# A graph layer's edge loop on one Trainium2 core: one stretch of the node table per two blocks, edge lists laid out two blocks to a row

## What is computed

```python
dst = jnp.minimum((6250 * uniform(100000) ** 2.0).astype(int32), 49999)   # then sorted; src permuted alike
row, col = edge_index[0], edge_index[1]                                  # src, dst
msg_in = concatenate([node_features[row], node_features[col]], axis=-1)
h = relu(msg_in @ Wm1 + bm1)
h = relu(h @ Wm2 + bm2)
messages = h @ Wm3 + bm3
agg = segment_sum(messages, col, 6250) / clip(count, 1.0)[:, None]
node_in = concatenate([node_features, agg], axis=-1)
upd = relu(node_in @ Wn1 + bn1) @ Wn2 + bn2
x = layernorm(x + node_features + upd)
```

## Time and profile before

| | |
|---|---|
| device time, median of 3 runs | 1201.61 us (1199.98 to 1201.78) |
| the profiled execution, first to last instruction | 1416.6 us |
| TensorE busy / VectorE / ScalarE / GpSimd | 88% / 69% / 52% / 56% |
| first transpose of the edge loop, last one | 89.4 us, 1308.2 us |
| moved by DMA | 211.42 MB, mean 149 GB/s |

### The profile page before, as it was taken

The page is one execution under the profiler, slowest core; times in us unless marked ns, Lnnn a source line. Parts: engine busy times, 40 slices in busy tenths (PEclk is TensorE's granted clock), DMA queues, the critical chain, the costliest instruction groups (busy, mean ns, idle before and its releaser), DMA issues.

```text
span 1416.6 us, 33766 instructions
## 1 busy us (share of the span) xinstructions
PE 1249.7 (88%) x9614; PEld 1172.0 (83%) x9615; DVE 979.6 (69%) x2072; ACT 740.6 (52%) x1392; POOL 786.5 (56%) x814
## 2 busy tenths in 40 slices
PE   6978888888888888888888889988999989899997
PEld 6868888888888888888888888888888888888886
DVE  6846666766766666766766766767767767777676
ACT  3544555555555555555555555555554555545585
POOL 2166666666666666666666666666666666564000
PEclk9999999999999999999999999999999999999999
DMA  9665555545545555555545555455545454554022
GB/s 308 274 234 156 146 144 151 149 141 151 151 140 150 152 142 147 151 143 147 152 139 150 146 143 151 145 144 152 139 147 151 138 150 144 145 151 142 10 67 86
DMA packets 135605, 211.42 MB, mean 149 GB/s; under 512 B 24247, under 2 KB 102669, under 8 KB 134030
## 3 DMA queue, kind: packets, MB, share of 16 engines
q1 hardware_dynamic: 98030, 108.43, 25.3%
q0 software_dynamic: 37536, 102.55, 25.1%
HBM read 188.09 MB, written 22.80 MB: 149 GB/s over the span
## 4 chain that ended last, share of the span: by engine, by line
PE 80%; issue 12%; DVE 2%; SPq 1%; another core or an unknown queue 1%; DMA 1%; ACT 1%; DVEq 1%; ACTq 0%
PE bank L1437 39%; PE bank L1413 11%; PE bank L1324 6%; PE sums L1345 4%; PE sums L1341 4%; PE sums L1347 3%; PE sums L1349 3%; PE bank L1478 2%; PE sums L1491 1%; PE bank L1234 1%; PE bank L1219 1%; PE bank L1461 1%; PE sums L1219 1%; DMA b_win<-b_table 1%
## 5 line engine op out<-in xcount | busy, mean ns | idle before, releaser
L630 POOL DMA_INDIRECT a_edge<-a_table,src_idx x782 | 767.1, 981 | 457.8 <-remote 268.2
L1437 PE MATMUL bank<-w,h 128*128 128x256 f32 x4692 | 661.4, 283 | 104.9 <-issue 102.1
L1437 PEld LDWEIGHTS bank<-w,h 128*128 128x128 f32 x4692 | 596.5, 188 | 119.7 <-issue 118.7
L1106 DVE SCALAR_TENSOR_TENSOR h<-bank,h 128x512 fp32r<-128x512 f32 x391 | 268.7, 687 | 338.4 <-issue 326.7
L732 ACT ACTIVATE h<-bank 128x512 fp32r<-128x512 f32 x391 | 233.8, 598 | 475.3 <-remote 439.2
L721 ACT COPY bank<-b_bc 128x512 f32<-128x512 f32 x391 | 231.5, 592 | 115.2 <-issue 66.7
L1118 DVE SCALAR_TENSOR_TENSOR h_lo<-bank,h_hi 128x512 fp32r<-128x512 f32 x391 | 266.5, 681 | 0.1
L1413 PE MATMUL bank<-ident,a_edge 128*128 128x128 f32 x1564 | 237.4, 274 | 21.1 <-issue 16.6
L740 ACT ACTIVATE h_hi<-bank 128x512 fp32r<-128x512 f32 x391 | 232.6, 595 | 2.8 <-PE bank L1437 2.8
L1413 PEld LDWEIGHTS bank<-ident,a_edge 128*128 128x128 f32 x1564 | 180.3, 140 | 40.5 <-issue 34.2
L1324 PE MATMUL bank<-onehot_t,b_win 128*128 128x256 f32 x782 | 190.3, 325 | 0.0
(11 more groups left out here) (190 smaller groups left out, 682.7 us busy)
## 6 DMA issues: line engine op xcount, KB each, us to landing
b_win<-b_table SPq DMA_DIRECT2D x391, 128.0 KB
rel<-rel_dram SPq DMA_DIRECT2D x196, 128.0 KB
a_edge<-a_table,src_idx POOLq DMA_INDIRECT x782
a_table<-work SPq DMA_DIRECT2D x12, 512.0 KB, 4.6
b_table<-work SPq DMA_DIRECT2D x5, 1024.0 KB
b_table<-h SPq DMA_DIRECT2D x4, 1024.0 KB
f_x<-in_x SPq DMA_DIRECT2D x12, 256.0 KB, 5.2
b_table<-a_edge SPq DMA_DIRECT2D x3, 1024.0 KB, 5.8
```

The source lines that it names most:

```text
L630: pool.indirect_dma_start(a_edge[:, b % R * TB + t, :], None, a_table, bass.IndirectOffsetOnAxis(ap=src_idx[:, b * TB + t:b * TB + t + 1], ...
L1106: dve.scalar_tensor_tensor(h1[:, k % U, 1, :], bank[k % 2][:, :], 0.0, h1[:, k % U, 0, :].bitcast(F32), ALU.max, ALU.subtract).then_inc(s_ ...
L1437: ins = pe.matmul(to, h1[:, j, a, h * EB + t * P:h * EB + (t + 1) * P], w2[:, b, h, :], start=False, stop=(a == 1 and h == KH - 1), skip_g ...
```

## The change

Two blocks share one window, which begins at the lower of their two lowest nodes. `b_win` is loaded once a pair, both blocks' relative numbers are taken from the pair's lowest node, and `far` of a block is counted from there too. In front of the loop the edge lists stand two blocks to a row: rows of 2 x 256 edges, in two column groups instead of four, so the loads and the stores of minima, maxima and relative numbers are fewer and their rows twice as long. VectorE makes the pair's minimum in two places (one on 98 x 2 and one on 1 x 392), and GpSimd's two fills of the padding are twice as wide.

```diff
-        full = E // EB
-        assert (GR - 1) * BG <= full
+        full = E // (2 * EB)
+        assert (GR // 2 - 1) * BG <= full < GR // 2 * BG
         loads = []
         for n in range(2):
-            for g in range(GR):
-                rows = min(full - g * BG, BG)
+            for a in range(GR // 2):
+                rows = min(full - a * BG, BG)
                 if rows:
-                    loads.append((n, g, 0, rows, EB))
-            if E % EB:
-                loads.append((n, GR - 1, rows, 1, E % EB))
+                    loads.append((n, a, 0, rows, 2 * EB))
+            if E % (2 * EB):
+                loads.append((n, GR // 2 - 1, rows, 1, E % (2 * EB)))
...
             def body(i):
-                first = load_words(sp, words_sp, i * U, U, PAD_DST)
-                for k in range(U):
-                    if there(i, k - RB):
-                        sp.wait_ge(s_ex, i * U + (k - RB + (2 if k % 2 == 0 else 1)))
-                    if k % 2 == 0:
-                        sp.dma_start(rel[:, k // 2, :].rearrange("p (b e) -> p b e", b=2),
-                                     rel_dram[bass.ds(i * U + k, 2), :].partition_broadcast(P)
-                                     ).then_inc(s_rc[k // 2], 16)
-                    if there(i, k):
-                        sp.dma_start(b_win[:, k % RB, :].bitcast(F32),
-                                     b_table[bass.ds(first[k] * 2, P), :]).then_inc(s_bw[k % RB], 16)
+                first = load_words(sp, words_sp, i * (U // 2), U // 2, PAD_DST)
+                for c in range(RC):
+                    if there(i, 2 * c - U):
+                        sp.wait_ge(s_ex, i * U + (2 * c - U + 2))
+                    sp.dma_start(rel[:, c, :].rearrange("p (b e) -> p b e", b=2),
+                                 rel_dram[bass.ds(i * U + 2 * c, 2), :].partition_broadcast(P)
+                                 ).then_inc(s_rc[c], 16)
+                    sp.dma_start(b_win[:, c, :].bitcast(F32),
+                                 b_table[bass.ds(first[c] * 2, P), :]).then_inc(s_bw[c], 16)
...
                 if k % 2 == 0:
                     dve.wait_ge(s_rc[k // 2 % RC], nth(i, k, 16))
-                dve.wait_ge(s_bw[k % RB], nth(i, k, 16))
+                    dve.wait_ge(s_bw[k // 2 % RC], nth(i, k, 16))
                 dve.wait_ge(s_g[k % R], nth(i, k, 16 * TB))
...
-                dve.tensor_tensor(far, highest, lowest, ALU.subtract).then_inc(s_rw, 1)
+                dve.wait_ge(s_low, 1)
+                dve.tensor_tensor(far, highest, row_low[0:1, :], ALU.subtract).then_inc(s_rw, 1)
...
-                    expand(b_win[:, k % RB, :], onehot_t[:, k % 2, :], k).then_inc(s_ex, 1)
+                    expand(b_win[:, k // 2 % RC, :], onehot_t[:, k % 2, :], k).then_inc(s_ex, 1)
```

More of the change, by code:

```diff
@@ L184, in gnn_layer @@
         minmax_i = carve(2 * GR).bitcast(I32)
+        pair_low = carve(GR // 2)
         first_quarter = carve(GR).bitcast(I32)
@@ L233, in gnn_layer @@
         s_mm = sem("s_min_max")
+        s_low = sem("s_lowest_of_pairs")
         s_wi = sem("s_min_max_int")
@@ L261, in gnn_layer @@
         s_rc = [sem(f"s_rel_loaded{c}") for c in range(RC)]
-        s_bw = [sem(f"s_b_win_loaded{c}") for c in range(RB)]
+        s_bw = [sem(f"s_b_win_loaded{c}") for c in range(RC)]
         s_bf = sem("s_b_far_loaded")
@@ L476, in _ @@
             sp.wait_ge(s_pad, 2)
-            for n, g, row, rows, edges in loads:
-                at, e0 = (n * GR + g) * EB, (g * BG + row) * EB
+            for n, a, row, rows, edges in loads:
+                at, e0 = (n * GR + 2 * a) * EB, (a * BG + row) * 2 * EB
                 sp.dma_start(edges_in[row:row + rows, at:at + edges],
@@ L516, in _ @@
                     sp.wait_ge(s_wi, 1)
-                    for j in range(GR):
-                        sp.dma_start(mm_dram[j * BG:(j + 1) * BG, :], minmax_i[0:BG, 2 * j:2 * j + 2]
-                                     ).then_inc(s_scr, 16)
+                    for a in range(GR // 2):
+                        sp.dma_start(mm_dram[a * 2 * BG:(a + 1) * 2 * BG, :].rearrange("(p c) m -> p (c m)", c=2),
+                                     minmax_i[0:BG, 4 * a:4 * a + 4]).then_inc(s_scr, 16)
                 if g == 4:
-                    sp.wait_ge(s_scr, 16 * GR)
+                    sp.wait_ge(s_scr, 16 * (GR // 2))
                     sp.dma_start(row_in[0:1, :], mm_dram.rearrange("(o b) c -> o (b c)", o=1)).then_inc(s_row, 16)
@@ L524, in _ @@
                     sp.wait_ge(s_rel16, 1)
[L525 to L529, removed]
+                    for a in range(GR // 2):
+                        sp.dma_start(rel_dram[a * 2 * BG:(a + 1) * 2 * BG, :].rearrange("(p c) e -> p (c e)", c=2),
+                                     rel16[0:BG, a * 2 * EB:(a + 1) * 2 * EB]).then_inc(s_scr_rel, 16)
+            sp.wait_ge(s_scr_rel, 16 * (GR // 2))
             sp.wait_ge(s_bz, 16)
@@ L891, in ranges_and_spans @@
                 dve.tensor_single_scalar(row_quarter[0:1, :], lowest, 5, ALU.arith_shift_right).then_inc(s_rw, 1)
-                dve.tensor_copy(words_sp[0:1, :], lowest).then_inc(s_rw, 1)
-                dve.tensor_tensor(far, highest, lowest, ALU.subtract).then_inc(s_rw, 1)
+                dve.tensor_tensor(words_sp[0:1, :], row_in[0:1, 0:2 * NB:4], row_in[0:1, 2:2 * NB:4], ALU.min
+                                  ).then_inc(s_rw, 1)
+                dve.tensor_tensor(row_low[0:1, :].rearrange("o (b c) -> o b c", c=2),
+                                  row_in[0:1, 0:2 * NB:4].unsqueeze(2).to_broadcast([1, NB // 2, 2]),
+                                  row_in[0:1, 2:2 * NB:4].unsqueeze(2).to_broadcast([1, NB // 2, 2]), ALU.min
+                                  ).then_inc(s_low, 1)
+                dve.wait_ge(s_low, 1)
+                dve.tensor_tensor(far, highest, row_low[0:1, :], ALU.subtract).then_inc(s_rw, 1)
                 dve.wait_ge(s_rw, 3)
@@ L902, in first_words @@
                 dve.wait_ge(s_rw, 6)
-                dve.scalar_tensor_tensor(words_act[0:1, 0:NB], far, float(2**13), lowest, ALU.mult, ALU.add
+                dve.scalar_tensor_tensor(words_act[0:1, 0:NB], far, float(2**13), row_low[0:1, :], ALU.mult, ALU.add
                                          ).then_inc(s_rw, 1)
```

20 lines of the change are left out of this document (13 added, 7 removed).

## The result

| | before | after |
|---|---|---|
| time, median of runs on the same chip (us) | 1201.69 (1199.98 to 1201.94, 4 runs) | **1227.15** (1225.71 to 1229.85, 4 runs) |
| ratio, 95% interval | 1 | 1.0213 [1.0198, 1.0229] |
| span of the profiled execution (us) | 1416.6 in the first recording, 1200.8 in a second one (run `e0_before_again`) | 1225.4 |
| first transposes of the loop (us) | 89.4 and 89.9 | 103.5 |
| packets, MB moved | 135605, 211.42 | 107033, 186.24 |

What follows compares the result with a forecast made beforehand. It took the plain loop to be paced by TensorE, at 2.574 us a block. Loop start -0.4, far blocks +7.5 and edge loads +15.5 made +22.6 us on 1201.6, so 1224 us, range 1212 to 1233.

Steps and rivals of the forecast that it cites:

- The edge loads, +15.5 taken: Prologue: the 97-row loads go over one DMA engine, so edge lists come late; +15.5 us, bounds 0 and 20.
- Both roads lead to the same shift: Prologue: late edge lists (some 15 us) and the late first `a_table` store (about 16 us) give the same delay.
- The 1.7 us of SyncE's issues are then worth nothing: Prologue: four fewer SyncE issues, 1.7 us, gain nothing since the queue's engine and not the issue is late.
- 1207: Rival: 97 rows spread, so the start gains 1.7 us while far blocks still cost 7.5; 1207 us, chance 0.07.
- The rival of 1196: Rival: loads spread, far blocks covered, plain loop waited for windows, at most 5.5 us back; 1196 us, chance 0.05.
- 1202.5: Rival, nothing measurable: loads spread and far blocks cost 1 us each; 1202.5 us, chance 0.04.
- The far blocks, 3 x 2.5 = 7.5 taken: Loop's tail, blocks 383, 387, 389: TensorE stands for `b_far`, 2.5 us each, 7.5 us; bounds 0.7 and 12.
- far blocks covered: Rival, loop's tail: ScalarE issues early enough, `b_far` lands in time, 1 us for each; 1219.7 us, chance 0.2.
- The windows, 0 taken, bounds 0 and 5.5: Loop: 195 fewer window loads gain 0 us, as the one-hot hardly waits for them; bounds 0 and 5.5.
- The loop start, -0.4: Start of the loop: the second one-hot no longer waits for a second window, about 0.4 us gained.
- The recording: Loop: recording adds 0.55 us a block to the profile's 3.125 us; a plain run takes 2.574 us.
- The sum: Whole kernel: -0.4 + 7.5 + 15.5 = +22.6 us, 1224.2 us against the plain median; chance 0.56.

Runs made afterwards that it cites:

- e0: The kernel before, unchanged, profiled once more: 1202.86 us, ratio 1.001, span 1200.8 us.
- e1: The kernel after, with each list's 97-row load split into 96 rows and 1 row: 1213.67 us, ratio 1.0102.
- e2: The kernel before, with its 1 KB rows, and only the first load of each edge list cut into 97 rows and one: 1209.63 us, ratio 1.0066.
- e9: The kernel after, with the two 97-row loads issued by ScalarE on its own queue at the start: 1232.87 us, ratio 1.0254.
- e6: The kernel before, with the change's edge lists (loaded as 96 and 1 rows) but the old windows, waits and far blocks: 1204.69 us, ratio 1.0021.
- e3: e1 with no block taken as far, leaving out three blocks' nodes beyond the window: 1205.0 us, ratio 1.002.
- e4: e1 with ScalarE loading the far window two blocks ahead instead of one: 1214.69 us, ratio 1.0104.
- e7: e4 with VectorE making the far one-hot right behind the ordinary one-hot of two blocks ahead: 1208.08 us, ratio 1.005.
- e5: e1 with each window loaded a second time into spare buffers and both loads waited for: 1217.55 us, ratio 1.0132.

## Why the prediction was right, and where not

**The edge loads, +15.5 taken.** The loop started 14.1 us later than in the earlier trace rows, 13.6 later than in e0. Mechanism and place were as forecast: shares of 0.06 to 0.07, the cast at 25.9 (27 forecast), L991 at 37.4 (38), the loop at 103.5 (105). The term was 10% too large. It took 21 to 24 GB/s for an engine from the earlier trace rows, that is from 16 engines at once and from rows of 512 bytes; alone with 2 KB rows one engine moved 25 to 26, and 371 thousand bytes at 26 GB/s are 14.3 us, what the first cast was late by (14.4). The rule of the Trainium skill that stood behind the reading (DMA: Bandwidth & Descriptors, "Why a DMA increments its semaphore by 16 and not by 1") is borne out for 97 rows by e1 and e2: one engine's share, 0.06 to 0.07, with 97, and 1.06 to 1.09 with 96 and one.

**"Both roads lead to the same shift."** Right. In the kernel after VectorE came to L991 of group 2 14.6 us later than in e0 and the store it waits for landed 13.9 us later, so the two ended within 1.8 us of each other, the store last. Had the store been on time, the step would have come some 12 us late instead of 13.9. In e9 the casts' road ended last and gave a still larger shift.

**"The 1.7 us of SyncE's issues are then worth nothing."** True of the kernel after, but the two rivals that added them as a gain for spread loads (1207 and 1196) had its sign wrong: with 96 and 1 rows (e6) the new lists cost 2 us and gain none. The rival of 1196 also took covered far blocks at 2 us, where 1219.7 and 1202.5 take them at 3.

**The far blocks, 3 x 2.5 = 7.5 taken.** They cost 10.0 us in the kernel after, of which some 0.9 are the fallen clock, and 8.4 in e1 (8.7 by the medians of e1 and e3). The count of three was right and so was the size of one stall, about 2 us of idle TensorE. That the size came out is in part luck, for the step behind it was incomplete: the working followed only ScalarE's issue and the landing of `b_far`. The DMA takes 2.3 to 3.4 us, less than the 3.59 of the earlier trace rows; it explains 3.5 of the 5.2 us of stalls in e1, and is last in one block of three. VectorE's one-hot at the end of its turn is last in the other two (4.3 of 5.8 us in the kernel after), and where the DMA was last the one-hot was close behind it (e4: no gain from an earlier load; e7: the stall gone). What is late next, once ScalarE's load is early, was not followed on to VectorE. Also mis-sized was the price of the work itself, 0.24 us for two matmuls "behind a loop's branches": in e7 it was 3.7 us for three blocks, 3.1 without the stalls that are left, about 1 us each. And the fall of the clock behind a stall was not thought of. (In the 2.3 us until TensorE needs `b_far`, the 0.43 for the transposes is 0.35 by the earlier trace rows; it changes nothing.) The rival "far blocks covered" (1219.7) had its condition wrong for the same reason: an early `b_far` alone covers nothing.

**The windows, 0 taken, bounds 0 and 5.5.** Right: 946.7 against 947.0 us over 368 blocks, 2.573 us a block in each, and e3 and e6 0.3 us apart. The 0.014 us a block between 2.56 and 2.574 that had been left as a possible gain is how a body of four is made: mostly 10.28 or 10.30 us, that is 2.57, 2.57, 2.58 and 2.56 or a little more, in e0 and e1 alike. The one-hot waited for windows much more than the 1.6 us of the earlier trace rows, 36 us in e0, 46 after, and from 15 (e7) to 54 (e6) in others with the same loop time, so that row was a poor argument, and by it the term came out right with some luck: in the stretched recording these loads were hardly ever late. The conclusion held because TensorE does not wait for that wait.

**The loop start, -0.4.** Not seen: it is below the 2.3 us by which recordings differ there, and no run has it alone.

**The recording.** The claim that a plain run takes 2.574 us a block, and that the first recording's 3.125 are no property of the kernel, was borne out by e0 (2.573).

**The sum.** 22.6 forecast, 24.6 by the recordings: -1.5 at the loop's start (13.6 against 15.5 - 0.4), +2.5 in the far blocks, and +1.1 in the three other stretches of the table (0.8 - 0.3 + 0.6). Some 1.5 us of it, in the far blocks and the rest, are the fallen clock; the 0.8 and the -0.3 were not traced. The errors partly cancelled: the loop's start was taken too large and the far blocks too small. The medians are 25.5 apart, another 0.9 us, within their scatter.

## What to carry to other kernels

Before a load's shape is changed, look at its row count: 97 rows, a prime number, put the whole transfer on one DMA engine, and what is queued for that engine on either queue comes late; one more issue for each list, which leaves 96 rows, took 13.5 us back. SyncE's loads in the loop fell by a third (587 to 392) and that gained nothing, since the engine that bounds the loop did not wait for them. The rare special case bought with it has a price per occurrence, and where two producers are both late, as `b_far` and its one-hot were, moving the load alone gained nothing. Of a recording that is much longer than the plain runs, as this one was, trust the busy times and the order, and none of its short waits. And a link of the chain that ended last is inferred: before building on it, check which group the named instruction belongs to and whether the waiting engine was idle at all.

## What was unexpected

- One recording of the same kernel took 1416.6 us and another 1200.8; they reached the loop at 89.4 and 89.9 us, and all but 1.5 us of the extra lay in it.
- Behind a load on one engine the issues themselves block: 3.34 and 7.50 us for single-row loads, and in e9 4.39 us for ScalarE's second issue and 9.5 us for two of SyncE's.
- Giving the long load a queue of its own made it end 8.1 us later (34.0 against 25.9 us), when the other queue's transfers had a share of its engine from the start.
- TensorE's granted clock was 0.50 through the idle prologue of the kernel after, up to 36 us by the windows. In the tail it fell during a stall of 2.57 us in e5, and in the kernel after some 1.7 us after one of 2.04 us had ended, while stalls of 2.29 us in the kernel after and of 2.00 and 2.03 us in e1 and e4 left it at 1.00. What decides between them no run here shows.
